# Two transformer blocks on one core: LayerNorm steps of block 1 moved between ticks, its transposes moved behind the output projection, one copy moved to the end of the tick

## The reference, cut to what matters

```
block 0:  x += attn(adaln(x))            16 heads of 16, self
          x += attn(adaln(x), ctx)       16 heads of 16, keys and values from ctx as it is
          x += W2 gelu(W1 adaln(x))      hidden 1024
block 1:  x += attn(adaln(x))            16 heads of 64 with rotary positions, self
          x += attn(adaln(x), ln(ctx))   16 heads of 64 with rotary positions, keys and values
                                         from the context after a LayerNorm over its 192 features
          x += f2 gelu(f1 adaln(x))      hidden 1024
adaln(x) = (x - mean) / sqrt(var + 1e-5) * w * (1 + scale(cond)) + b * (1 + scale) + shift(cond)
attn     = softmax(q k^T / sqrt(d)) v, then an output projection
```

## Time and profile before

| | us |
|---|---|
| median of 3 executions | 4402.54 |
| the profiled execution | 4394.15 |
| its span, first to last instruction | 4392.0 |
| TensorE matmul busy | 4145.6 (94%) |
| VectorE busy | 2959.7 (67%) |
| ScalarE busy | 2745.7 (63%) |
| GpSimd busy | 2758.7 (63%) |

### The profile page before, as it was taken

The page is one execution under the profiler, slowest core; times in us unless marked ns, Lnnn a source line. Parts: engine busy times, 40 slices in busy tenths (PEclk is TensorE's granted clock), DMA queues, the critical chain, the costliest instruction groups (busy, mean ns, idle before and its releaser), DMA issues.

```text
span 4392.0 us, 95934 instructions
## 1 busy us (share of the span) xinstructions
PE 4145.6 (94%) x34934; PEld 3514.9 (80%) x34934; DVE 2959.7 (67%) x6250; ACT 2745.7 (63%) x10788; POOL 2758.7 (63%) x2555
## 2 busy tenths in 40 slices
PE   7999989888889999999999999999999999999999
PEld 5777777777779987888888888778787878787998
DVE  7999988889865556555556565666666666665443
ACT  5999888888863335656565666656565656564332
POOL 4666666666667775555555565666666666665776
PEclk9999999999999999999999999999999999999999
DMA  2110011111111122222222222322222222221110
GB/s 74 33 33 30 31 41 37 45 45 36 44 55 49 40 73 80 73 75 73 73 75 73 73 78 86 101 75 85 74 86 74 86 73 86 74 91 61 49 46 33
DMA packets 229269, 276.65 MB, mean 63 GB/s; under 512 B 37948, under 2 KB 160320, under 8 KB 228800
## 3 DMA queue, kind: packets, MB, share of 16 engines
q1 hardware_dynamic: 228732, 270.51, 18.0%
q10 hardware_dynamic: 68, 0.02, 0.0%
HBM read 85.89 MB, written 50.33 MB: 31 GB/s over the span
## 4 chain that ended last, share of the span: by engine, by line
PE 65%; DVE 20%; ACT 8%; issue 5%; POOL 2%; DMA 0%; ACTq 0%; SPq 0%; POOLq 0%; DVEq 0%
PE BANKS L573 15%; PE BANKS L575 14%; PE BANKS L574 14%; PE BANKS L724 6%; PE BANKS L712 6%; PE BANKS L760 5%; DVE NM L995 4%; DVE PT L1002 3%; ACT PR L880 2%; ACT PR L864 2%; DVE WL L1044 1%; DVE Z L1101 1%; ACT HF L908 1%; DVE ST L1091 1%; PE BANKS L769 1%
## 5 line engine op out<-in xcount | busy, mean ns | idle before, releaser
L1180 POOL TENSOR_TENSOR PR<-PR,RL 128x512 f32<-128x512 f32 x1024 | 1069.5, 1045 | 946.0 <-DVE RL L1007 942.5
L880 ACT ACTIVATE PR<-BANKS,NM 128x128 f32<-128x128 f32 x2048 | 730.0, 384 | 487.8 <-DVE NM L1058 431.0
L864 ACT ACTIVATE PR<-BANKS,NM 128x128 f32<-128x128 f32 x2048 | 728.9, 415 | 3.9 <-DVE NM L995 3.8
L573 PE MATMUL BANKS<-HH,WH 128*128 128x512 f32 x1632 | 691.7, 424 | 38.0 <-DVE SN L1072 26.7
L1058 DVE TENSOR_REDUCE NM<-BANKS 128x8 f32<-128x1024 f32 x256 | 312.7, 1222 | 532.2 <-PE BANKS L724 532.1
L760 PE MATMUL BANKS<-ID,PR 128*128 128x128 f32 x4096 | 632.9, 278 | 40.6 <-DVE OL L1051 22.8
L575 PE MATMUL BANKS<-HH,WL 128*128 128x512 f32 x1632 | 644.5, 395 | 0.0
L574 PE MATMUL BANKS<-HL,WH 128*128 128x512 f32 x1632 | 644.2, 395 | 0.0
L760 PEld LDWEIGHTS BANKS<-ID,PR 128*128 128x128 f32 x4096 | 496.0, 142 | 165.1 <-issue 61.9
L864 ACT ACTIVATION_READ_ACCUMULATOR PR<-BANKS,NM 128x1 f32 x2048 | 520.1, 257 | 0.0
L1203 POOL TENSOR_TENSOR GL<-GF,GH 128x512 fp32r<-128x512 f32 x256 | 342.4, 1338 | 206.1 <-DVE GH L1147 206.1
(11 more groups left out here) (123 smaller groups left out, 10825.9 us busy)
## 6 DMA issues: line engine op xcount, KB each, us to landing
SW<-SN SPq DMA_DIRECT2D x1024, 128.0 KB, 2.0
x_scratch<-X SPq DMA_DIRECT2D x80, 512.0 KB, 3.2
X<-x_scratch SPq DMA_DIRECT2D x80, 512.0 KB, 4.0
CX<-in_ctx SPq DMA_DIRECT2D x32, 384.0 KB, 4.2
X<-in_x SPq DMA_DIRECT2D x16, 512.0 KB, 3.8
out<-X SPq DMA_DIRECT2D x16, 512.0 KB, 2.9
CX<-in_ctx SPq DMA_DIRECT2D x32, 128.0 KB, 3.8
STG<-in_L_xcond_W SPq DMA_DIRECT2D x4, 512.0 KB, 5.0
```

What stands on the lines that cost most here:

```text
L573: e.matmul(o, lh, rh, start=first and i == 0, stop=False)
L864: made = e.activation(pr[:, r], bank[:, r], ACT.Exp, bias=nm[:, h:h + 1], accum_out=RL[npr(t)[0]][:, h:h + 1])
L880: made = e.activation(pr[:, r], bank[:, r], ACT.Exp, bias=nm[:, h:h + 1], accum_out=RL[npr(t)[0]][:, h:h + 1])
L1180: e.tensor_tensor(p3, p3, RL[npr(t)[0]][:, :].unsqueeze(2).broadcast_to([128, 4, 128]), ALU.mult).then_inc(s_nrm, 1)
```

## The change

No instruction is added or left out. Stages are put into other ticks, and two places in the programs of the engines change.

- Kind b: x is loaded 21 ticks ahead of tg and not 17. The four stats go from ticks -13, -13, -12, -12 to -18, -18, -17, -17; root from -12 to -16; the four norms from -11, -11, -10, -10 to -15, -14, -13, -12. The two turns (with hf) go from -9 and -8 to -11 and -9, the splits from -8 and -7 to -10 and -8.
- Context of pass 4: c_stats from -13, -13, -12, -12 to -14, -14, -13, -13; c_norm from -11, -11, -10, -10 to -11, -10, -9, -8; both c_turn and c_hf from -8 and -7 to -7; both c_split from -7 and -6 to -6.
- TensorE: turn and c_turn stand behind out in a tick and no longer ahead of it.
- VectorE: c_merge stands behind c_split in a tick and no longer ahead of the rotary multiplies. This holds for pass 1 too, where it was ahead of v_out (line 1023).

```diff
-            at["load_x", tg - {"a": 40, "b": 17, "f": 14}[kind]].append((p, g))
-            norm = tg - {"a": 26, "b": 10, "f": 8}[kind]
+            at["load_x", tg - {"a": 40, "b": 21, "f": 14}[kind]].append((p, g))
+            norm = tg - {"a": 26, "b": 12, "f": 8}[kind]
             turn = norm + {"a": 2, "b": 1, "f": 2}[kind]
...
+            elif kind == "b":
+                for b in range(G):
+                    at["stats", norm - 6 + b // 2].append(Batch(p, g, b))
+                    at["norm", norm - 3 + b].append(Batch(p, g, b))
+                at["root", norm - 4].append((p, g))
...
+            apart = 2 if kind in "ab" else 1
             for c in range(2):
                 for i in range(parts):
-                    at["turn", turn + parts * c + i].append(Part(p, g, c, i))
-                    at["hf", turn + parts * c + i + (p < 3)].append(Part(p, g, c, i))
-                at["split", turn + parts * c + parts + (p < 3)].append(Part(p, g, c, 0))
+                    at["turn", turn + apart * c + i].append(Part(p, g, c, i))
+                    at["hf", turn + apart * c + i + (p < 3)].append(Part(p, g, c, i))
+                at["split", turn + apart * c + parts + (p < 3)].append(Part(p, g, c, 0))
...
-                        at["c_stats", tg - 13 + b // 2].append(Batch(p, g, b))
-                        at["c_norm", tg - 11 + b // 2].append(Batch(p, g, b))
+                        at["c_stats", tg - 14 + b // 2].append(Batch(p, g, b))
+                        at["c_norm", tg - 11 + b].append(Batch(p, g, b))
...
-                    at["c_turn", tg - (14 if p == 1 else 8) + c].append(Part(p, g, c, 0))
-                    at["c_hf", tg - (13 if p == 1 else 8) + c].append(Part(p, g, c, 0))
-                    at["c_split", tg - (12 if p == 1 else 7) + c].append(Part(p, g, c, 0))
+                    at["c_turn", tg - 14 + c if p == 1 else tg - 7].append(Part(p, g, c, 0))
+                    at["c_hf", tg - 13 + c if p == 1 else tg - 7].append(Part(p, g, c, 0))
+                    at["c_split", tg - 12 + c if p == 1 else tg - 6].append(Part(p, g, c, 0))
```

More of the change, by code:

```diff
@@ L761, in _ @@
                     made.then_inc(s_t, 1)
+                for x in at["out", tick]:
+                    key, k = ("co" if x.p == 4 else "so"), x.i % 2
+                    wh, wl = wview(WH, key), wview(WL, key)
+                    q.wait_ge(s_ol, o_use(x) + 1)
+                    if x.j == 0:
+                        q.wait_ge(s_zr, 1)
+                        for i in range(2):
+                            q.wait_ge(*tp.free(("y", x.p, x.g, i)))
+                            e.matmul(PS[6 + i][:, :].rearrange("p (r t) -> p r t", r=4), ZR[:, :], ZR[:, :].unsqueeze(1).broadcast_to([128, 4, 128]),
+                                     start=True, stop=False)
+                    q.wait_ge(s_wlo, w_ready[key])
+                    for b in range(G):
+                        made = three(PS[6 + b // 2][:, 256 * (b % 2):256 * (b % 2) + 256],
+                                     [(OH1[k][:, b, :], OL1[k][:, b, :], wh[:, x.j, :], wl[:, x.j, :])], False, x.j == 7 and b % 2 == 1)
+                    made.then_inc(s_y, 1)
                 for x in at["turn", tick]:
@@ L781, in _ @@
                     made.then_inc(s_turn, 1)
[L783 to L797, removed]
                 for p, g, j in at["up", tick]:
@@ L1007, in _ @@
                     e.reciprocal(rl[:, :], rl[:, :]).then_inc(s_rl, 1)
[L1009 to L1012, removed]
                 for x in at["v_out", tick]:
@@ L1140, in _ @@
                     e.tensor_copy(HH[k][:, x.c, :], HF[u % 2][:, x.c, :]).then_inc(s_hh, 1)
+                for p, g in at["c_merge", tick]:
+                    u, k = h_of(p, g, True)
+                    q.wait_ge(s_hl, 2 * u + 2)
+                    e.tensor_copy(HH[k][64:128, 1, :], HL[k][64:128, 1, :].bitcast(F)).then_inc(s_hm, 1)
                 for p, g, j in at["up", tick]:
```

## The result

The kernel before took 4400.02 us (median of 4 runs, 4395.08 to 4405.3), the changed one 4303.16 us (4 runs, 4298.31 to 4308.35). The ratio is 0.978, with a 95% interval of 0.9763 to 0.9797: 97 us faster, where 81 were forecast.

The account below looks back on a forecast made before the run. The prediction took TensorE to bound passes 3 and 4, pass 1 being another case. Savings of 15 (pass 3), 61 (pass 4) and 5 (pass 1), 81 us, from 4402.5 gave 4321 us, range 4298 to 4362.

Parts of the forecast that it names:

- rival 2: Pass 1: with k's wait shorter, the granted clock falls less often; up to 20 us more saved, 4301 us; chance 0.10.
- Pass 3: Pass 3: TensorE's waits at the turns and v1 vanish, group 72.34 to 71.31 us; 15 us saved, bounds 0 and 15.
- the 1.03: Pass 3: the us a group that is wait, 0.51 of it ahead of v1; all taken away by the new order.
- Pass 4: Pass 4: 4.25 us of wait a group goes, 0.45 comes back; 61 us saved over 16 groups, bounds 47 and 68.
- the norms at 1.31: Pass 4: TensorE's 1.31 us bracket ahead of q1, put down to VectorE's adds, norms and c_norms making `max` late.
- The step that compared whole units with quiet ones: Pass 4: the two units with turns take 23.17 us together, against 16.72 for quiet ones; 6.45 us longer.
- The new wait ahead of scores: Pass 4, once a group: scores wait for GpSimd's key rotary add behind two subtractions; 0.45 us, bounds 0 and 1.3.
- Pass 1: Pass 1: c_merge moved, so V fills VectorE's idle time and k starts 0.3 us sooner; 5 us saved, bounds -4 and 7.
- Rival 1: Pass 4: GpSimd's pile in tick -6 costs the full 1.3 us and `max` stays late; 4352 us; chance 0.15.
- Rival 4: Whole kernel: waits come from the round of three banks and return in full elsewhere; 4402 us; chance 0.04.
- Rival 3: Passes 3 and 4: moved VectorE instructions each lose 1.0 us to GpSimd, 220 us; 4541 without idle cover; chance 0.05.

Follow-up runs that it names:

- Experiment 3: The changed kernel with TensorE's turn and c_turn back ahead of out, ticks as changed; 4342.12 us, ratio 0.9871.
- Experiment 4: The kernel before with x of block 1 loaded earlier and its stats, root and norms spread, turns where they were; 4372.65 us, ratio 0.9942.
- Experiment 2: The changed kernel with c_merge put back ahead of v_out; 4325.93 us, ratio 0.9831.
- Experiment 5: The changed kernel with GpSimd's subtractions (split, c_split) behind its rotary adds in a tick; 4298.22 us, ratio 0.9772.
- experiment 1: The kernel before with only c_merge moved, to the end of its tick on VectorE; 4386.01 us, ratio 0.9968.
- experiment 6: The changed kernel with c_turn, c_hf, c_split and c_merge of pass 1 one tick earlier; 4297.07 us, ratio 0.9765.
- experiment 7: The changed kernel with both GpSimd's subtractions behind its rotary adds and pass 1's four context stages one tick earlier; 4290.17 us, ratio 0.9745.

## Why the prediction was right

The 97 us lie past the forecast's own upper bound of 95 and within the stated range only because that took in rival 2. Passes 3 and 4 came within 3 us of their terms by the mechanism that was told; pass 1 didn't, and brings 10 of the 16 us that were missing.

*Pass 3.* 15 us forecast, 15.7 measured; the group came to 71.27 where the working gave 71.31. Experiment 3 divides the 1.03: with the turns in odd ticks but ahead of out, 0.56 of them stay. So about half is the place in the tick, and about half the tick (the norms, spread alone in experiment 4, leave the group at 72.30).

*Pass 4.* 61 us forecast, 63.3 measured. Experiment 4 gives the spread norms 1.64 us a group, and experiment 3 gives the place behind out 2.05; the sum is 3.69 of the 3.89. Experiment 2 adds 0.14 for c_merge, which the working had at nothing in this pass. The working had the norms at 1.31, since it took the bracket for the whole. It isn't: the bracket of the turn behind shrank by 0.10 with it, and the rest stood in no bracket. The step that compared whole units with quiet ones (23.17 against 16.72) had caught it, so only the division by cause was off, not the sum.

*The new wait ahead of scores.* Forecast 0.45 us once a group, in the place given; measured 0.32. Experiment 5 takes it away by the order of GpSimd's queue alone and gains 0.38 a group. That the turn behind out costs 0.42 as work agrees as well: the unit that holds it in pass 4 lasts 3037.74 - 3028.94 = 8.80 us, a quiet one of this trace 8.35, 0.45 less.

*Pass 1.* This is the term that was mis-sized: 5 us forecast, 14.8 measured, over the bound of 7. The mechanism and the order of instructions were right. Two things were off. First, k starts 0.10 us after the copy ends (853.32 + 1.15 = 854.47, against 854.57), where 0.2 had been taken, and the copy took 1.15 us and not 1.25. In spite of a norm of 0.52 us and not 0.4 ahead of it, k's wait shrank by 0.52 and not by 0.3: 14 x 0.52 = 7.3 us over the 14 groups that were summed above. Secondly, the clock. Rival 2 said that it would fall less often, and that is the other 7.2 us of these groups (16.9 - 9.7). So rival 2 was true beside the forecast, with a third of its 20 us, and the objection to it, that an eighth of a wait is little, doesn't hold.

The 7.2 are of one pair of profiles, though. Over 14 groups the falls cost 9.7 to 17.2 us in the five profiles whose pass 1 runs the order of the changed kernel, and 16.9 to 19.8 in the three that run that of before; the two spans overlap at their ends, and their means differ by 6. Over all profiles, the time between 610 and 1210 us that is spent at 1.2 GHz goes with k's wait: 61 to 72 us in the three kernels where it is 2.7 us (before, experiments 2 and 4), 41 to 58 in the five profiles where it is 2.2 (the changed kernel twice, experiments 1, 3 and 5), and 17 in the two where it is 1.5 (experiments 6 and 7). The granted clock of every execution, not only of the profiled ones, has the same order: its median is 0.985 to 0.987 where the wait is 2.7 us, 0.988 to 0.989 where it is 2.2, and 0.993 where it is 1.5. The spread within the middle five may be why c_merge alone gave 12 to 14 us in experiment 1 and taking it back cost 23 in experiment 2; that isn't shown. That the shorter wait is the cause, and not something else that came with it, is argued from this order and not shown: no run set the wait by itself.

*Rival 1, the queue in front of scores,* failed by its size: the pile cost 0.32, not 1.3, and `max` was in time. *Rival 4, no change:* both kernels share the same three banks, and the waits didn't come back elsewhere. By experiment 3 the place in the tick covers them, all but the half of pass 3 that the ticks give.

*Rival 3, VectorE and GpSimd shutting each other out.* The mechanism is there, but its price fell into VectorE's idle time. Timelines of VectorE and then of GpSimd in pass 4 of the changed kernel:

```profile
3025.96 0.41 DVE L1102 TENSOR_SCALAR Z<-X,MV,RS 128x256 f32<-128x256 f32 x1
...
3028.47 1.42 DVE L1102 TENSOR_SCALAR Z<-X,MV,RS 128x256 f32<-128x256 f32 x1
```

```profile
3027.46 1.04 POOL L1186 TENSOR_TENSOR PR<-PR,RL 128x512 f32<-128x512 f32 x1 [1.98 <-DVE RL L1013]
3028.45 1.28 POOL L1203 TENSOR_TENSOR QT<-QT,SW 128x512 f32<-128x512 f32 x1
```

A norm takes 0.41 us while GpSimd is idle (its 1.98 us of idle end at 3027.46) and the next one 1.42 when its start, at 3028.47, comes 0.02 after that of a GpSimd instruction that ends at 3029.73. By the rule of the Trainium skill, page "SBUF — State Buffer", section "Who interferes with whom", a VectorE instruction on both ports and a GpSimd instruction exclude each other. The trace agrees, with 1.42 against 0.41, though the long norm ends only 0.16 us after the GpSimd instruction. It costs about the 1.0 us that the rival assumed, but at one norm of four in pass 4 (13 of 52 in 13 groups) and at none in pass 3: VectorE's busy time rises by 23 us in all (2959.7 to 2982.7), not by 220. And it stays hidden: without waits the groups of passes 3 and 4 come to the 71.3 and 69.1 us that were worked out with no such cost. Pass 1 has little cover, with 94% in experiment 6.

## What to carry to other kernels

Before an in-order queue is reordered, measure a stage from one start of a marker to the next and subtract the quiet stages; the difference is the whole wait, of which the bracket ahead of q1 showed 1.31 of 1.6 us. Put work that needs a buffer just released behind work that doesn't, in the same stage: the matmuls of out between were worth 37 to 39 of the 97 us here. Where another engine is busy 94% of a stage, to move its work can just move the waits, as in experiment 6; what remains to try there is less work or fewer collisions between VectorE and GpSimd.

## What the runs showed of the hardware that was not expected

The granted clock in pass 1 falls in some groups and not in others though they run the same instructions: in the changed kernel 40.01 us at a mean clock of 0.91 and the next group 38.29 at 1.00, with waits of k of 2.17 us ahead of both. It fell in 10 or 11 of 14 groups with waits of 2.7 us (three profiles), in 6 to 9 with 2.2 (five), in 4 or 5 with 1.5 (two). What picks the groups was not tried and stays open. It is worth between 5.3 us (experiment 7) and 19.8 (experiment 2) over the same 14 groups, as much as an edit, and it moved by 7.5 us (9.7 to 17.2, the changed kernel and experiment 3) with no change to pass 1 at all.

A copy of half the partitions took 1.15 us in the changed kernel, beside a GpSimd instruction, and 0.42 in experiment 6, where GpSimd stood idle from 846.67 to 848.27. So 0.7 of the 1.15 come with the GpSimd instruction beside it.

From the end of VectorE's instruction to the start of the TensorE matmul that waited for it 0.10 us passed here (854.47 to 854.57), and 0.15 in the kernel before (851.86 + 0.49 against 852.50); 0.2 had been taken.
